# A decoder layer on one core: the first two steps of the recurrence pipeline get orders of their own on PE, ACT and DVE

## What is computed

```python
xx = shifted(x) - x                                  # x is layer-normed
a = tanh((x + xx * maa_x) @ maa_w1)                  # 5 groups of 32 columns
mw, mk, mv, mr, mg = einsum(a, maa_w2)               # one mix each
xw = x + xx * (maa_w + mw)                           # xk, xv, xr, xg alike
r, k, v, g = xr @ W_r.T, xk @ W_k.T, xv @ W_v.T, silu(xg @ W_g.T)
w = time_decay + tanh(xw @ decay_w1) @ decay_w2
y = wkv6(r, k, v, w, u)                              # S = exp(-exp(w)) * S + k v^T, per token
out = (groupnorm(y) * gamma + beta) * g @ W_o.T
```

## Time and profile before

| | us |
|---|---|
| median of three runs | 875.16 |
| the profiled execution | 875.0 |
| its span | 873.2 |
| PE busy (share) | 827.3 (95%) |
| DVE busy (share) | 738.1 (85%) |
| ACT busy (share) | 505.0 (58%) |
| granted clock of PE, mean | 0.98 |

### The profile page before, as it was taken

One profiled execution on the slowest core, in us unless ns is written; L12 is line 12 of the kernel. 1 busy time (PEld: TensorE's weight loads), 2 busy tenths in 40 slices (PEclk: granted clock), 3 DMA queues, 4 the chain that ended last, 5 costly groups with the idle time before them and its releaser, 6 DMA issues.

```text
span 873.2 us, 23820 instructions
## 1 busy us (share of the span) xinstructions
PE 827.3 (95%) x10117; PEld 666.5 (76%) x10134; DVE 738.1 (85%) x1206; ACT 505.0 (58%) x728; POOL 139.1 (16%) x197
## 2 busy tenths in 40 slices
PE   7898999999999999999889999999999978999997
PEld 6798988888898888889777788888888845444453
DVE  5987989899898989986575689889888979999995
ACT  5566372846546374643535436435444457999995
POOL 1001020100102010100102000000000123676441
PEclk9899999999999999999879999999999989999999
DMA  8330112030211202023140340430232120242311
GB/s 256 126 110 19 44 34 90 15 110 15 69 44 50 75 14 86 15 86 108 65 170 2 146 162 8 146 144 29 115 144 97 39 98 25 87 143 98 109 67 55
DMA packets 36553, 72.41 MB, mean 83 GB/s; under 512 B 6081, under 2 KB 6977, under 8 KB 35433
## 3 DMA queue, kind: packets, MB, share of 16 engines
q1 hardware_dynamic: 35912, 68.93, 23.9%
q0 software_dynamic: 544, 2.10, 0.6%
HBM read 58.39 MB, written 12.58 MB: 81 GB/s over the span
## 4 chain that ended last, share of the span: by engine, by line
PE 72%; DVE 16%; issue 5%; POOL 4%; ACT 1%; DMA 1%; DVEq 0%; POOLq 0%; SPq 0%; ACTq 0%
PE P L62 11%; PE P L63 9%; PE P L64 9%; PE S L750 6%; PE S L2290 5%; PE P L2276 4%; POOL sm L378 3%; DVE xf L1026 3%; DVE E L1862 2%; PE S L636 2%; PE S L1723 2%; PE S L62 2%; PE S L63 2%; PE S L64 2%; PE S L1710 2%
## 5 line engine op out<-in xcount | busy, mean ns | idle before, releaser
L378 POOL TENSOR_TENSOR sm<-sm,mhalf 128x16 f32<-128x16 f32 x8 | 30.6, 3828 | 303.7 <-DVE sm L1121 303.7
L2290 PE MATMUL S<-wq,hqT 128*128 128x512 bf16 x255 | 59.9, 380 | 2.6 <-ACT hqT L2214 2.2
L750 PE MATMUL S<-R,K 64*64 64x32 f32 x3072 | 57.2, 223 | 2.8 <-DVE K L1072 1.7
L750 PEld LDWEIGHTS S<-R,K 64*64 64x64 f32 x3072 | 51.5, 137 | 10.4 <-issue 4.7
L2276 PE MATMUL P<-wq,xqT 128*128 128x512 bf16 x240 | 56.1, 387 | 2.3 <-ACT xqT L2192 1.2
L1862 DVE TENSOR_SCALAR E<-S,upper 128x2048 f32<-128x2048 f32 x16 | 37.6, 2349 | 24.2 <-PE S L1710 24.0
L1536 ACT ACTIVATE E<-E 128x2048 f32<-128x2048 f32 x16 | 30.6, 1913 | 45.3 <-DVE E L1862 45.3
L1868 DVE RECIPROCAL rec<-S 128x512 f32<-128x512 f32 x16 | 53.6, 3350 | 1.8 <-PE S L1725 1.8
L1026 DVE TENSOR_TENSOR xf<-P,xx 128x1024 f32<-128x1024 f32 x40 | 48.7, 1218 | 7.3 <-PE P L657 7.2
L1033 DVE TENSOR_TENSOR xf<-xf,xnT 128x1024 f32<-128x1024 f32 x40 | 49.1, 1227 | 1.1
L2276 PEld LDWEIGHTS P<-wq,xqT 128*128 128x128 bf16 x256 | 24.7, 100 | 29.3 <-issue 2.7
(11 more groups left out here) (300 smaller groups left out, 2701.0 us busy)
## 6 DMA issues: line engine op xcount, KB each, us to landing
wch<-in_wff SPq DMA_DIRECT2D x32, 256.0 KB, 3.1
cwch<-in_wff SPq DMA_DIRECT2D x8, 1024.0 KB, 7.0
xt<-in_x SPq DMA_DIRECT2D x8, 512.0 KB, 4.5
y<-in_x SPq DMA_DIRECT2D x8, 512.0 KB, 3.6
out<-y SPq DMA_DIRECT2D x8, 512.0 KB, 3.3
cxt<-out SPq DMA_DIRECT2D x8, 512.0 KB, 4.1
ct<-in_ctx SPq DMA_DIRECT2D x8, 512.0 KB, 5.1
cxr<-out SPq DMA_DIRECT2D x8, 512.0 KB, 7.0
```

Source lines behind the costliest of these rows:

```text
L378: pool.tensor_tensor(sm[:, 2, :], sm[:, 1, :], mhalf[:, 0:2 * H], ALU.pow).then_inc(y_rstd, 1)
L750: mm = pe.matmul(ps[half_rows(side), par, b, k, :], K[head_rows(par), r % 2, at:at + HALF], right_tokens(par, g, side, i), start=True, sto ...
L2290: mm = pe.matmul(O[:, :], hqT[b % 2][:, k, :], w2q[:, k, :], start=k == 0, stop=k == NF - 1)
```

## The change

Steps 1 and 2 leave `step` on ACT, PE and DVE and become `first_step` and `second_step`, straight lists; pieces of the old `step` become functions with their waits unchanged (`copy_turned`, `copy_k`, `copy_r`, `copy_v`, `tanh_g`, `exps`, `decay_tanh`, `normalize`, `gate`, `decay_in`, `decay_out`, `turn_in`). Each of the three loads of W2 has a semaphore of its own, and its low half is split in three places (`low_w2`). SP's order of loads follows. The quarters of the token shift wait one by one. In all steps the stack's rows are copied in another order. The core of the difference, without the moved functions:

```diff
 # sync, step
             if p is not None:
-                if p == 0:
-                    sp.wait_ge(w2_lo, 3)
-                    sp.dma_start(chunks(stage["g"]), weights_v["g"]).then_inc(wload["g"], 16)
+                if q == 0:
+                    sp.wait_ge(wsplit_lo, 3)
+                    sp.dma_start(chunks(stage["o"]), weights_v["o"]).then_inc(wload["o"], 16)
                 load_part(p, 0)
+                load_part(p, 1)
                 if p == 0:
                     sp.wait_ge(wsplit_lo, 1)
                     sp.dma_start(chunks(stage["v"]), weights_v["v"]).then_inc(wload["v"], 16)
-                load_part(p, 1)
...
+                    sp.wait_ge(w2_lo, 3)
+                    sp.dma_start(chunks(stage["g"]), weights_v["g"]).then_inc(wload["g"], 16)
                 load_part(p, 2)
 # scalar
             stack_rows(0, 0)
             stack_rows(0, 2 * D_MIX)
-            for j in range(1, 4):
+            stack_rows(1, 0)
+            stack_rows(1, 2 * D_MIX)
+
+        def stack_middle(p):
+            for j in range(2, 4):
                 stack_rows(j, 0)
+        def first_step():
+            copy_turned(0)
+            for i, (raw, j0, j1) in enumerate(w2_pieces):
+                act.wait_ge(w2_in[i], 16)
...
+            stack_first(0)
+            stack_middle(0)
+            narrow_tanh(0)
+            stack_second(0)
+            stack_last(0)
+            decay_tanh(0)
+            split_weight("k")
+            abs_sum(0, 0)
+            hi(0, 1)
+            split_weight("r")
+            abs_sum(0, 1)
+            hi(0, 2)
+            hi(0, 3)
+            normalize(1)
+        def second_step():
+            hi(0, 4)
+            copy_turned(1)
+            high_v(0)
+            high_v(1)
+            stack_first(1)
+            copy_k(0)
+            narrow_tanh(1)
+            stack_middle(1)
+            stack_second(1)
+            stack_last(1)
+            abs_sum(0, 2)
+            copy_r(0)
+            decay_tanh(1)
+            hi(1, 1)
+            split_weight("g")
+            abs_sum(0, 3)
+            copy_v(0)
+            hi(1, 2)
+            exps(0)
+            split_weight("o")
+            normalize(2)
+            tanh_g(0)
+            hi(1, 3)
+            abs_sum(1, 0)
+            abs_sum(1, 1)
+            abs_sum(1, 2)
+            abs_sum(1, 3)
 # tensor
         def mix(p, j, ps):
+            if p == 0:
+                pe.wait_ge(w2_lo, (1, 1, 2, 3, 3)[j])
             if j == 0:
                 if p == 0:
-                    pe.wait_ge(w2_lo, 3)
                     pe.wait_ge(ones_ready, 1)
-                pe.wait_ge(a_tanh, 5 * (p + 1))
+                pe.wait_ge(a_tanh, 5 * (p + 1) if p > 0 else 1)
...
+        def token_shift(p):
+            for k in range(NC):
+                pe.wait_ge(xxx_ready, NC * p + k + 1)
+                mm = pe.matmul(X1[:, 0:2 * T], w1[:, k, 0:4 * D_MIX], xf[0][:, k, :], start=k == 0, stop=k == NC - 1)
+            mm.then_inc(a_done, 1)
+        def first_step():
+            keep_busy(X2, 8)
+            turn_in(0)
+            keep_busy(X2, 12)
...
+            token_shift(0)
+            narrow(0, None)
+            keep_busy(L, 3)
+            mix(0, 0, X0)
+            keep_busy(L, 6)
...
+            mix(0, 1, X0)
+            keep_busy(L, 2)
...
+            decay_in(0)
+            pe.wait_ge(mix_ready, 2)
+            mix(0, 2, X0)
+            pe.wait_ge(a_tanh, 5)
+            keep_busy(X2, 20)
...
+            channel_major("k", X0, 0)
+            mix(0, 3, X1)
+            channel_major("k", X0, 1)
+            channel_major("k", X0, 2)
+            pe.wait_ge(mix_ready, 4)
+            mix(0, 4, X1)
+            channel_major("k", X0, 3).then_inc(k_done, 1)
+        def second_step():
+            pe.wait_ge(wload["v"], 16)
+            centre_v(0)
+            turn_in(1)
+            pe.wait_ge(aw_ready, 1)
+            centre_v(1)
+            pe.wait_ge(xnT_ready, 2)
+            keep_busy(X1, 2)
+            token_shift(1)
+            keep_busy(X1[:, C:2 * C], 4)
+            narrow(1, 0)
...
+            channel_major("r", X1, 2)
+            channel_major("r", X1, 3)
+            mix(1, 0, X0)
+            channel_major("r", X1, 0)
+            pe.wait_ge(mix_ready, 6)
+            mix(1, 1, X0)
+            channel_major("r", X1, 1).then_inc(r_done, 1)
+            decay_in(1)
+            pe.wait_ge(mix_ready, 7)
+            mix(1, 2, X0)
+            mix_3(1, 0)
+            pe.wait_ge(wsplit_lo, 3)
+            keep_busy(X2, 4)
...
+            token_major("v", half["v"], X0, 0)
+            token_major("v", half["v"], X0, 1).then_inc(v_done, 1)
+            pe.wait_ge(aw_ready, 2)
+            decay_out(0)
...
+            channel_major("g", X0, 0)
+            pe.wait_ge(mix_ready, 9)
+            mix(1, 4, X1)
+            for m in range(1, NC):
+                mm = channel_major("g", X0, m)
+            mm.then_inc(g_done, 1)
                  if r == 0:
-                    keep_busy(X2, 10)
+                    turn_in(p)
+                    keep_busy(X2, 2)
 # vector
+        def first_step():
+            shift(0)
+            maa_x(0)
+            low_w2(0)
+            lower_stack(0, 0, 2)
+            mix(0, 0)
+            xf_sum(0, 0)
+            mix(0, 1)
+            low_w2(1)
+            lower_stack(0, 2, 4)
+            lower_g(0)
+            xf_sum(0, 1)
+            mix(0, 2)
+            split_weight("k")
+            lo(0, 1)
+            norm(1)
+            low_w2(2)
+            xf_sum(0, 2)
+            mix(0, 3)
+            norm_shift(1)
+            xf_sum(0, 3)
+            lo(0, 2)
+            mix(0, 4)
+        def second_step():
+            xf_sum(0, 4)
+            lo(0, 3)
+            shift(1)
+            maa_x(1)
+            split_weight("r")
+            lo(0, 4)
+            lower_stack(1, 0, 2)
+            low_v(0)
+            low_v(1)
+            mix(1, 0)
+            lower_stack(1, 2, 4)
+            xf_sum(1, 0)
+            mix(1, 1)
+            lower_g(1)
+            xf_sum(1, 1)
+            rk(0)
+            mix(1, 2)
+            split_weight("g")
+            lo(1, 1)
+            xf_sum(1, 2)
+            mix(1, 3)
+            xf_sum(1, 3)
+            norm(2)
+            prepare()
+            lo(1, 2)
+            mix(1, 4)
+            norm_shift(2)
+            split_weight("o")
+            gate(0)
+            lo(1, 3)
+            xf_sum(1, 4)
```

More of the change, by code:

```diff
@@ L170, in rwkv_parts @@
     g_stacked = sem("g_stacked")
-    w2_in = sem("w2_in")
+    w2_in = [sem(f"w2_in{i}") for i in range(3)]
     w2_hi, w2_lo = sem("w2_hi"), sem("w2_lo")
@@ L382, in step @@
             if n == 0:
-                pool.wait_ge(w2_in, 3 * 16)
+                for i in range(3):
+                    pool.wait_ge(w2_in[i], 16)
                 for w in "kr":
@@ L490, in step @@
             if f:
[L491 to L504, removed]
-            if s_:
[L506 to L515, removed]
+                copy_turned(p)
+                abs_sum(p, 0)
+            if s_:
+                copy_k(q)
             if f:
                 stack_first(p)
+                stack_middle(p)
                 narrow_tanh(p)
@@ L612, in step @@
             if n is not None:
[L613 to L615 removed]
+                normalize(n)
             if f:
                 abs_sum(p, 3)
[L618 to L619 removed]
             if last_levels(q, r):
@@ new lines, in decay_in, with decay_out @@
+        def decay_in(p):
+            pe.wait_ge(xf_ready, 5 * p + 1)
+            for k in range(NC):
+                for b in range(2):
+                    mm = pe.matmul(L[D_DECAY * b:D_DECAY * b + D_DECAY, 0:T], wd1[:, k, :],
+                                   xf[1][:, k, T * b:T * b + T], start=k == 0, stop=k == NC - 1)
+            mm.then_inc(wd1_done, 1)
+        def decay_out(q):
+            for k in range(NC):
+                for b in range(2):
+                    rows = slice(D_DECAY * b, D_DECAY * b + D_DECAY)
+                    mm = pe.matmul(L[:, C * b + T * k:C * b + T * k + T], wd2[rows, P * k:P * k + P], aw[q % 2][rows, :], start=True, stop=True)
+            mm.then_inc(wd2_done, 1)
@@ L914, in step @@
                 pe.wait_ge(aw_ready, p + 1 if f else q + 1)
-                for k in range(NC):
-                    for b in range(2):
-                        rows = slice(D_DECAY * b, D_DECAY * b + D_DECAY)
-                        mm = pe.matmul(L[:, C * b + T * k:C * b + T * k + T], wd2[rows, P * k:P * k + P], aw[q % 2][rows, :], start=True, stop=True)
-                mm.then_inc(wd2_done, 1)
-                if f and t_:
+                decay_out(q)
+                if f:
                     mix_3(p, q)
-                if q == 0:
-                    pe.wait_ge(wsplit_lo, 3)
-                    keep_busy(X2, 14)
                 pe.wait_ge(lo_ready, 4 * q + 2)
@@ L1149, in prepare, with gate, low_w2 @@
```

(12 more changed lines are left out.)

305 lines of the change are left out of this document (140 added, 165 removed).

## The result

The changed kernel takes 883.58 us (median of 4 runs, 882.42 to 884.59); the kernel before took 875.2 beside it. The ratio is 1.0093, with a 95% interval of 1.0076 to 1.011: slower, by 8.4 us where 4.1 were forecast, and outside the range that ended at 882.8. Profiled execution against profiled execution it is 882.7 against 875.0, +7.7 us; the spans, 880.9 and 873.2, differ by the same.

What follows compares the result with a forecast made beforehand. The start of level 0 of the first recurrence was taken to bound the kernel, PE being full behind it: 875.0 + 2.5 (level 0 later) + 1.8 (clock behind the stall) = 879.3 us, range 875.8 to 882.8.

Steps and rivals of the forecast that it cites:

- what bounds, and the place: PE is full from 89 us on, so the change is worth its shift of the first recurrence's level 0 (88.09 us).
- Behind it: Gate's tanh to level 0: four sums sharing `wch` wait three transfers of 3.0 us; level 0 at 90.6, +2.5 us.
- Up to the gate's tanh: First two steps: the new orders bring the gate's tanh to 74.2 from 79.49 us, 5.3 us sooner.
- main case: Level 0 2.5 us later plus 1.8 us for the clock behind the stall: 879.3 us, chance 0.47.
- rival 4: First two steps: PE drops to half clock behind idle patches, 2.5 us on top: 881.8 us, chance 0.18.
- The clock: Behind PE's 10 us stall at level 0: some 5 us at half speed, +1.8 us net, bounds 0 and 2.7.
- later steps: Six later steps, one row copy moved ahead of the narrow tanh: 0 taken, 0.6 us as bound.
- The sign given for being wrong: Steps from 140 us on that differ by more than 0.1 us each would show the prediction wrong.

Runs made afterwards that it cites:

- Experiments one: Changed kernel with the six late sums of `wch` spread over idle places of ACT's second step: 872.91 us, ratio 0.9954.
- three: Kernel before with pair 1's four sums in one row behind x_g's high half and SP's W_o load ahead of the pieces: 882.93 us, ratio 1.0097.
- experiment six: Changed kernel with sums spread, more fillers in step 2 and DVE's ones behind the first norm's shift: 869.24 us, ratio 0.9941.
- experiment seven: The changed kernel itself measured once more, no new edit: 885.66 us, ratio 1.0112.
- experiments two: Changed kernel with 14 instead of 4 fillers behind step 2's token shift and 9 more ahead of mix 3: 883.59 us, ratio 1.0083.
- ten: Changed kernel with sums spread and 19 more fillers in step 2, DVE's ones left in place: 870.63 us, ratio 0.993.
- experiment eleven: Changed kernel with sums spread, fillers in step 2 and DVE's ones behind the norm's shift, measured once more: 869.76 us, ratio 0.9924.
- nine: Changed kernel with only the sums spread over ACT's second step, measured once more: 871.59 us, ratio 0.994.
- experiment five: Changed kernel with DVE's ones of the stack written behind the first norm's shift: 884.34 us, one run, only its profile read.
- experiment four: Changed kernel with 40 fillers on PE ahead of level 1 of the first recurrence: 882.35 us, ratio 1.0068.

## Why the prediction was wrong, and where it was right

- **Right: what bounds, and the place.** Everything hung on when level 0 starts, and the delay there passed through five recurrences to within 0.25 us in the two executions compared; over the others five recurrences differ from before by -0.9 to +1.0 us.
- **Right: the step "Behind it".** Four sums through one buffer: three rounds as sized, 16.97 us in place of the forecast 16.4. The missing 0.57 is in the waits, 9.82 us with the last at 3.63; I had given all three 3.0. Experiments one and three show the cause from both sides: taking the pile away brings level 0 to 6.80 us behind the tanh, putting it into before costs 7.7.
- **Wrong: the step "Up to the gate's tanh", 5.3 us sooner.** It was 0. The step counted every row at the duration it has at full clock, and put the clock's loss on this way at nothing in the main case. Of the 5.28 us between 74.2 and 79.48, the two falls behind the idle patches took 3.03 (60.49 - 57.46). The late first product took 1.78 (18.99 against the 17.21 of experiment six): 0.55 by POOL's power, 0.87 by the turn into channels, 0.36 behind them. The last 0.47 is the sum's own error, the tanh of experiment six being at 74.67. By the prediction's own terms it is 0.67, for 73.5 and 0.5 are 74.0 and not 74.2; and ACT's 73.8 is 0.3 later than the products' 73.5, not "no later". I had written the patches down (rival 4: 2.1, 2.3 and 2 us idle, "fewer fillers around") and priced one fall at 2.5 with a chance of 0.18. The trace of before had shown one such patch and one such fall; that evidence called for a fall in the main case. How many falls was not to be read from it: the patch at 21 us brought none in the changed kernel, and the other two brought one or both. The prediction took durations from rows at full clock and then an order with less work around them: the durations did not carry over.
- **Size: "The clock" behind the stall, +1.8.** PE stalled for 10.49 us as forecast (10) and had the half clock after it. From level 0 to the first mark takes 28.40 us before and 28.51, 28.52, 28.51, 28.51 and 28.52 in the five executions without a stall, but 29.50 after, and 29.14 to 29.54 in five more with it, 31.75 in the sixth (experiment seven, clock 0.50 from 97 to 105 us). So 0.6 to 1.1 was usual and 3.3 possible, where 1.8 was forecast.
- **Right in the sum: later steps 0** (-0.25 over five). The sign given for being wrong, steps that differ by more than 0.1 us each, did appear (+0.26, +0.11, +0.63, -0.50, -0.75), but both ways: single steps vary by that much between executions, so it was no sign.
- **Not foreseen: the change to cross-attention.** From sixth to last mark it is 98.93 us before, 95.84 after and 97.52 to 101.94 in the eleven other executions, the program being alike there; PE's granted clock is another each time (in 445 to 460 us 0.73, 0.89, 0.66, 0.57 in before, after, experiments two and ten), though it does not order them alone (0.80 with 101.15 us in experiment eleven). So two executions of nearly one kernel differ by some 3 us. That is why the profiled execution shows 7.7 of the 8.36 + 1.10 that went in; the median's 8.4 cannot be taken apart in this way. It is not all luck, perhaps: experiments six, nine, ten and eleven, four of the five that reach the sixth mark soonest (361.91 to 367.51), need 100.16 to 101.94 there, all others at most 99.39. Then 1 to 2 us of an early gain would be given back at that place, and 1.5 to 4 us at level 0 would show as 0 to 3 in the medians. What decides it was not isolated; it stays open.

Added up with what was measured: 0 for the tanh, +8.4 for the sums, +1.1 for the clock behind: 9.5 us at the first mark, against the forecast 4.3.

## What to carry to other kernels

A chain "use, load, use" through one buffer costs a transfer's latency per round when it stands in a row on an engine that others wait for; the same four uses among other work of that engine cost nothing at the point the others wait for, and here that alone turned +0.93% into -0.46%, and -0.60% when repeated. Fillers belong to an order: when work is moved earlier, the idle time moves too, and what keeps the clock up has to be placed anew, behind the waits of the new order. A ledger built from rows is only as good as the state in which those rows ran: for each new idle patch, ask what clock the next rows would have.

## What was not expected of the hardware

- An idle patch of 2.40 or 2.15 us in PE's second step could be followed by a granted clock of 0.50 or 0.57, which cost 1.5 us each time. All six executions with the two patches had a fall behind one of them at least, three behind both; the five with fillers in them had none. In 23 to 31 us, with 2.10 and 3.08 of 4 us busy, the clock stayed at 1.00, where before it fell. With the same fillers the fall between 50 and 54 us came in the changed kernel and not in experiment five. The Trainium skill (TensorE: Matmul & The Clock Gate, The HAM clock gate) says that the point at which a kernel's first matmuls reach the full clock varies from run to run. Here the return to it behind the stall varied: the clock is 1.00 by 103 us in the changed kernel and still 0.50 in 103 to 105 in experiment seven.
- After 9.09 us of fillers, 1.61 us without work were followed by a granted clock of 0.50 some two us later (experiment four).
- POOL's 128x2 power takes 1.28 us beside a DVE `tensor_scalar` of 0.82 us that only touches two partitions, and 0.71 or 0.72 without it. The Trainium skill (GPSIMD Engine Reference, Key points) says that GpSimd shares its memory interfaces with VectorE and contends with instructions of VectorE that run in a 2-port mode or read two operands from SBUF. This one reads one; whether it ran in such a mode no row shows, and whether it is those ports was not tried.
